# A ring of three h slots and a product with a diagonal of B in the state-space scans of a two-layer Perceiver kernel

## The chip, the cores and the metric

The kernel runs on one core of a Trainium2 chip. Its time is the device time of one execution in microseconds: 3793.17 us as the median of three runs (3791.55, 3793.17, 3795.02). The engines are called PE (TensorE, with PEld for its weight loads), DVE (VectorE), ACT (ScalarE), POOL (GpSimd) and SP (SyncE, which issues the DMAs). Everything is fp32. PSUM is the memory that PE writes; SBUF is the working memory.

## The reference

Two layers, each of cross-attention, a state-space ("Mamba") block and a feed-forward block, over 16 x 64 = 1024 tokens of width 512. What matters here is the recurrence of the two state-space blocks, with 16 states n for each channel d and a restart at each of the 16 sequences of 64 tokens:

```
dA = exp(dt[..., None] * A)
dBx = dt[..., None] * B[:, :, None, :] * x[..., None]
def step(h, inp):
    dA_t, dBx_t, C_t = inp
    h = dA_t * h + dBx_t
    y = jnp.einsum('bdn,bn->bd', h, C_t)
    return (h, y)
y = ys + D * x
```

The block of layer 0 has 512 channels, that of layer 1 has 1024 channels (and multiplies y by a gate after it).

## The kernel before

Channels lie on the 128 partitions and tokens along the free axis. `scan_states` (L220) treats 512 channels, as CN = 4 chunks of 128. It is called three times: once for layer 0 (tile names BS_..., B_...), and for layer 1 once for each half of the channels (ES0 and ES1, shown as ES_..., E_... in the trace). These calls are named the first, second and third scan stage here.

One call runs through 64 steps, in the order half of the tokens (2, HALF = 512 tokens each), state n (16), pair of chunks cp (2). A step s treats W = 2 chunks of 512 tokens, so tiles of 128 x 1024, and goes through four engines:

- ACT makes `dA` = exp(delta * A) in two instructions (L291, 128 x 504 each). It also makes the tile `scaled`: du (that is dt * x), laid out with tokens on partitions in `duT`, times the column B of state n (L272, `times_b`). That is 4 pieces of 128 tokens x 512 channels for each state, which serve the two steps of the state; the list in L294 says how far ahead of the steps the pieces are issued, mostly two after each pair of exponentials.
- PE turns `scaled` back to channels on partitions with 8 transposes of 128 x 128 into the PSUM tile `dB` (`entering`, L365). `dB` has NE = 2 slots, so `entering(s)` waits for scan s-2 (`h_ready`).
- DVE scans: h = dA * h + dB over 1024 elements (`scan`, L329). It writes slot s mod NH of a ring of NH = 2 slots, so scan s waits until POOL has read slot s-2 (`hc_ready`).
- POOL multiplies h by the row C of state n (L315) into a ring `hc` of NP = 2 slots; its step s waits for scan s (`h_ready`) and for PE having added step s-2 (`summed`).
- PE adds `hc` into the PSUM tile `acc`, again with 8 transposes (`add`, L382), after `hc_ready`.

The order on PE is fixed: entering(s+2), then add(s-1). At the last state of each half (n = 15) `add` adds the skip term D * x too (8 more transposes), and DVE finishes the half (`finish`, L340 or L344); in layer 1 ACT copies `acc` out and PE turns it back first (L280, L392). POOL makes the skip terms (L306, four instructions) ahead of its first step. Both rings h and hc lie in the space of `du`, four chunks of 1024 tokens, whose values are no longer needed once `duT` is made.

Of the kernel before, what the change touches and what calls it, by code (L numbers as in the profile page):

```python
# [12 lines left out]
P = 128  # L13
# [180 lines left out]
N_STATE = 16  # L194
HALF = TOK // 2
# [24 lines left out]
def scan_states(nc, consts, tag, delta, du, duT, b_col, A, rows, q0, CN, skip, skip_col, finish_to, gate=None):  # L220

    with ExitStack() as stack:
        r = Region(nc, stack, tag)
        NH, NP, ND, NE, NS = 2, 2, 3, 2, 3
        W = 2
        CP = CN // W
        TILES = HALF // P
        acc = r.ps("acc", [P, CN, HALF])
        dB = r.ps("dB", [P, NE, W, HALF])
        dA = r.sb("dA", [P, ND, W, HALF])  # L230
        h = du[:, 0:2, :].rearrange("p k (w t) -> p k w t", w=W)
        hc = du[:, 2:4, :].rearrange("p k (w t) -> p k w t", w=W)
        scaled = r.sb("scaled", [P, NS, TILES, CN * P])
        yt = r.sb("yt", [P, W, HALF]) if gate is not None else None
        cleared, da_ready, skip_ready = r.sem("cleared"), r.sem("da_ready"), r.sem("skip_ready")
# [8 lines left out]
        def chunks(s):  # L244
            return range(W * STEPS[s][2], W * STEPS[s][2] + W)

        def tokens(tile, c, half):
            return tile[:, c, bass.ts(half, HALF)]

        def ring_q(half, n):  # L250
            return q0 + N_STATE * half + n

        def piece(m, i):
            t = TILES * (m // N_STATE) + i
            return scaled[:, m % NS, i, :], duT[:, t, :], b_col(t, m % N_STATE)

        with nc.Block() as block:
            @block.sync
            def _(sp):
                for k in range(2 * N_STATE):  # L260
                    q = q0 + k + NR
                    if q < rows.total:
                        sp.wait_ge(hc_ready, CP * (k + 1))
                        rows.load_c(sp, q)

            @block.scalar
            def _(act):
                def times_b(m, i):
                    if m >= NS and i == 0:
                        act.wait_ge(db_full, CP * (m - NS + 1))  # L270
                    to, of, col = piece(m, i)
                    nc.scalar.activation(to, of, ACT.Copy, scale=col).then_inc(scaled_ready, 1)  # L272
# [30 lines left out]
            @block.gpsimd  # L303
            def _(pool):
                for c in range(CN):
                    nc.gpsimd.tensor_scalar(skip[:, c, :], skip[:, c, :], skip_col(c), None, ALU.mult  # L306
                                            ).then_inc(skip_ready, 1)
                for s, (half, n, cp) in enumerate(STEPS):
                    q = ring_q(half, n)
                    pool.wait_ge(h_ready, s + 1)  # L310
                    if s >= NP:
                        pool.wait_ge(summed, s - NP + 1)
                    if cp == 0:
                        pool.wait_ge(rows.c_in[q % NR], 16 * (q // NR + 1))
                    nc.gpsimd.tensor_tensor(hc[:, s % NP], h[:, s % NH],  # L315
                                            rows.C[:, q % NR, :].unsqueeze(1).broadcast_to([P, W, HALF]), ALU.mult
                                            ).then_inc(hc_ready, 1)

# [36 lines left out]
            @block.tensor  # L355
            def _(pe):
                def entering(s):
                    half, n, cp = STEPS[s]
                    m = N_STATE * half + n
                    pe.wait_ge(scaled_ready, TILES * (m + 1))  # L360
                    if s >= NE:
                        pe.wait_ge(h_ready, s - NE + 1)
                    for j, c in enumerate(chunks(s)):
                        for i in range(TILES):
                            last = nc.tensor.transpose(dB[:, s % NE, j, bass.ts(i, P)], scaled[:, m % NS, i, bass.ts(c, P)],  # L365
                                                       consts["ident"][:, :])
                    last.then_inc(db_full, 1)

                def add(s):

                    half, n, cp = STEPS[s]
                    pe.wait_ge(hc_ready, s + 1)
                    if half and n == 0:
                        pe.wait_ge(finished, W * (nth_last[s - CP] + 1))
                    for j, c in enumerate(chunks(s)):
                        parts = [hc[:, s % NP, j, :]]
                        if n == N_STATE - 1:
                            pe.wait_ge(skip_ready, CN)
                            parts.append(tokens(skip, c, half))
                        for part in parts:  # L380
                            for i in range(TILES):
                                last = nc.tensor.matmul(acc[:, c, bass.ts(i, P)], part[:, bass.ts(i, P)],  # L382
                                                        consts["ident"][:, :], start=(n == 0 and i == 0),
                                                        stop=(n == N_STATE - 1), is_transpose=True,
                                                        skip_group_check=True)
                    last.then_inc(summed, 1)

                def turn_back(s):
                    for j, c in enumerate(chunks(s)):
                        pe.wait_ge(copied, W * nth_last[s] + j + 1)  # L390
                        for i in range(TILES):
                            last = nc.tensor.transpose(acc[:, c, bass.ts(i, P)], yt[:, j, bass.ts(i, P)],  # L392
                                                       consts["ident"][:, :])
                        last.then_inc(turned, 1)

                for s in range(NE):
                    entering(s)
                for s in range(len(STEPS) + 1):
                    if s + NE < len(STEPS):
                        entering(s + NE)  # L400
                    if s:
                        add(s - 1)
                    if gate is not None and s - 2 in nth_last:
                        turn_back(s - 2)
                for s in LASTS:
                    if gate is not None and s + 2 >= len(STEPS) + 1:
                        turn_back(s)
# [799 lines left out]
def l0_mamba(nc, consts, X, A_log, Dw, xproj, dtw, dtb, bc_scratch, ffn_weights, project):  # L1207
# [3 lines left out]
    with ExitStack() as stack:  # L1211
# [25 lines left out]
        with ExitStack() as inner:  # L1237
# [7 lines left out]
            with nc.Block() as block:  # L1245
# [68 lines left out]
                def _(act):  # L1314
# [19 lines left out]
            q.restart()  # L1334

        scan_states(nc, consts, "BS", delta, du, duT, lambda t, n: Bt[:, t, R + n:R + n + 1], A, rows, 0, CN, XnT,
                    lambda c: Dd[:, c:c + 1], X)
        r.restart()
# [1014 lines left out]
def l1_mamba(nc, consts, X, a, bc_scratch):  # L2353
# [7 lines left out]
    with ExitStack() as stack:  # L2361
# [271 lines left out]
        for g in range(C // CG):  # L2633
            with ExitStack() as inner:
# [11 lines left out]
                with ExitStack() as first:  # L2646
                    acc = first.enter_context(nc.psum_tensor(f"E3{g}_z", [P, CG, TOK], F32))
                    with nc.Block() as block:
# [57 lines left out]
                        def _(dve):  # L2706
# [18 lines left out]
                    q.restart()  # L2725
                chunk = slice(CG * g, CG * g + CG)
                scan_states(nc, consts, f"ES{g}", delta, du, duT, lambda t, n: pr[:, t, R + n:R + n + 1], A[:, chunk, :], rows, 2 * N_STATE * g, CG, U[:, chunk, :],
                            lambda c: cols[:, CG * g + c, Dcol:Dcol + 1], U[:, chunk, :], gate=Gt[:, chunk, :])

# [292 lines left out]
```

## Time and profile before

| | |
|---|---|
| median of three runs | 3793.17 us |
| profiled execution, its own time | 3795.1 us |
| its span | 3793.4 us |
| busy: PE, PEld, DVE, ACT, POOL | 3459.6, 2592.3, 2248.7, 1579.7, 1329.9 us |
| first scan stage, first to last step on POOL | 1100.0 to 1256.2 us |
| second scan stage | 3306.3 us to the last two steps, which start at 3462.15 us |
| third scan stage | 3508.05 to 3666.1 us |

The page gives busy times over the whole span; the attention stages, which the change does not touch, hold most of PE's. The three scan stages make up about an eighth of the span, and they have to be read by themselves, engine by engine. A timeline row merges like instructions that follow each other without a gap: "4.71 ... x2" is 4.71 us from the start of the first to the end of the second, so that the distance of their starts is 4.71 less the length of one. Instructions of an engine may overlap a little in this view: on ACT and PE the next one starts before the one before has ended.

### The profile page before, as it was taken

To read this page: it belongs to the slowest core of one execution; us is meant where nothing else is said; L and a number is where in the kernel's file an instruction comes from. 1 tells how busy PE (TensorE), PEld (TensorE's weight loads), DVE (VectorE), ACT (ScalarE), POOL (GpSimd) and SP (SyncE) were. 2 spreads that over 40 slices of the span, in tenths; PEclk is the share of its full clock that TensorE was granted. 3 is DMA by queue.
4 is the path that set the end of the run, shared out by engine and by line. 5 is a ranking of instruction groups with operands and counts; after the bars stand their busy time and mean duration, and the time that the engine had idled before them with its cause. 6 is when DMAs were issued, how large, how long until landed. Compare 5 with 4: busy or idle time off the path is not lost. (4 is left out here: it accounts for less than half of the span.)

```text
span 3793.4 us, 76745 instructions
## 1 busy us (share of the span) xinstructions
PE 3459.6 (91%) x33752; PEld 2592.3 (68%) x33752; DVE 2248.7 (59%) x2305; ACT 1579.7 (42%) x2169; POOL 1329.9 (35%) x652
## 2 busy tenths in 40 slices
PE   7999999999777689999999999999999998686788
PEld 4566666665247555888888888888888846575764
DVE  4677777777259842555555555555555415597972
ACT  2555555555279421222222222222222103698960
POOL 3344444442069421122222222222222004396961
PEclk9999999999779889999999999999999999798999
DMA  6455555553112042111111111111111112111110
GB/s 203 129 147 151 146 149 149 149 145 86 40 62 54 6 155 78 36 48 34 35 46 42 50 42 50 42 50 42 50 42 46 73 42 56 39 52 34 51 48 23
DMA packets 215251, 277.18 MB, mean 73 GB/s; under 512 B 67056, under 2 KB 165328, under 8 KB 213632
## 3 DMA queue, kind: packets, MB, share of 16 engines
q1 hardware_dynamic: 214920, 272.28, 24.8%
q8 instruction: 267, 4.37, 0.5%
q14 instruction: 64, 0.52, 0.0%
HBM read 218.63 MB, written 53.13 MB: 72 GB/s over the span
## 5 line engine op out<-in xcount | busy, mean ns | idle before, releaser
L1770 POOL TENSOR_TENSOR D_ctx_lo<-D_ctx_raw,D_ctx_hi 128x2048 fp32r<-128x2048 f32 (+1 forms) x64 | 270.0, 4219 | 1203.9 <-ACT D_ctx_hi L1764 1203.9
L730 DVE TENSOR_REDUCE A_mxc<-A_psX 128x2 f32<-128x768 f32 (+2 forms) x512 | 480.8, 983 | 115.5 <-PE A_psX L772 111.6
L1047 ACT ACTIVATE A_probs<-A_psE 128x1024 f32<-128x1024 f32 (+1 forms) x416 | 426.4, 1025 | 294.1 <-PE A_psE L1105 291.9
L1789 ACT ACTIVATE D_V<-D_psY 128x384 f32<-128x384 f32 x208 | 101.9, 490 | 890.0 <-PE D_psY L1855 890.0
L1805 DVE TENSOR_REDUCE D_mxc<-D_psE 128x4 f32<-128x1536 f32 (+2 forms) x128 | 241.9, 1890 | 204.3 <-PE D_psE L1883 204.3
L2146 ACT ACTIVATE D_probs<-D_psE 128x2048 f32<-128x2048 f32 x112 | 210.5, 1879 | 295.8 <-PE D_psE L2259 295.8
L329 DVE TENSOR_TENSOR_SCAN E_du<-ES_dA,ES_dB 128x1024 f32<-128x1024 f32 x128 | 292.3, 2285 | 39.0 <-POOL E_du L315 23.5
L2275 PE MATMUL D_psO<-D_probs,D_V 128*32 128x256 f32 (+1 forms) x5376 | 313.4, 381 | 0.0
L315 POOL TENSOR_TENSOR E_du<-E_du,E_Cn 128x1024 f32<-128x1024 f32 x128 | 301.7, 2373 | 19.2 <-DVE E_du L329 13.1
L1855 PE MATMUL D_psY<-D_wv_hi,D_ctx_hi 128*128 128x384 f32 x832 | 285.5, 343 | 0.0
L1845 PE MATMUL D_psY<-D_ctx_hi,D_wk_hi 128*128 128x384 f32 (+2 forms) x768 | 279.9, 364 | 0.0
L1855 PE MATMUL D_psY<-D_wv_hi,D_ctx_lo 128*128 128x384 f32 x832 | 279.1, 336 | 0.0
L1855 PE MATMUL D_psY<-D_wv_lo,D_ctx_hi 128*128 128x384 f32 x832 | 278.6, 335 | 0.0
L1845 PE MATMUL D_psY<-D_ctx_hi,D_wk_lo 128*128 128x384 f32 (+2 forms) x768 | 268.4, 350 | 0.0
L1845 PE MATMUL D_psY<-D_ctx_lo,D_wk_hi 128*128 128x384 f32 (+2 forms) x768 | 268.4, 349 | 0.0
L2186 DVE TENSOR_TENSOR D_acc<-D_acc,D_probs 128x1024 f32<-128x1024 f32 x96 | 135.7, 1414 | 213.5 <-ACT D_probs L2146 209.8
L2275 PEld LDWEIGHTS D_psO<-D_probs,D_V 128*32 128x32 f32 (+1 forms) x5376 | 163.5, 110 | 115.6 <-issue 9.0
L1105 PEld LDWEIGHTS A_psE<-A_Qst,A_Kst 50*128 50x128 f32 (+1 forms) x1664 | 123.0, 184 | 169.6 <-ACT A_probs L1047 117.4
L1105 PE MATMUL A_psE<-A_Qst,A_Kst 50*128 50x256 f32 (+1 forms) x1664 | 211.4, 333 | 24.9 <-ACT A_probs L1047 19.3
L1120 PE MATMUL A_psO<-A_probs,A_V 128*17 128x256 f32 (+1 forms) x3328 | 228.5, 389 | 0.2 <-ACT A_probs L1047 0.2
L2254 PE MATMUL D_psE<-D_Q_hi,D_K_hi 32*128 32x256 f32 (+1 forms) x2688 | 208.1, 294 | 5.7 <-PEq L49 5.7
L365 PE MATMUL ES_dB<-all_ident,ES_scaled 128*128 128x128 f32 x1024 | 143.0, 286 | 72.2 <-DVE E_du L329 63.6
(368 smaller groups left out, 7654.2 us busy)
## 6 DMA issues: line engine op xcount, KB each, us to landing
A_land<-in_ctx SPq DMA_DIRECT2D x32, 768.0 KB, 5.6
D_ctx_raw<-in_ctx SPq DMA_DIRECT2D x32, 768.0 KB, 4.6
A_land<-in_ctx SPq DMA_DIRECT2D x16, 1024.0 KB, 5.9
D_ctx_raw<-in_ctx SPq DMA_DIRECT2D x16, 1024.0 KB, 5.9
E_Cn<-bc_scratch SPq DMA_DIRECT2D x64, 256.0 KB, 3.3
k_scratch<-A_Khl SPq DMA_DIRECT2D x32, 384.0 KB, 4.3
A_Kst<-k_scratch SPq DMA_DIRECT2D x64, 192.0 KB, 3.5
A_land<-in_ctx SPq DMA_DIRECT2D x16, 642.0 KB, 4.3
```

What stands on the lines that cost most here:

```text
L315: nc.gpsimd.tensor_tensor(hc[:, s % NP], h[:, s % NH], rows.C[:, q % NR, :].unsqueeze(1).broadcast_to([P, W, HALF]), ALU.mult).then_inc(hc ...
L329: nc.vector.tensor_tensor_scan(h[:, s % NH].rearrange("p w t -> p (w t)"), dA[:, s % ND].rearrange("p w t -> p (w t)"), dB[:, s % NE].rear ...
L730: nc.vector.tensor_reduce(mxc[:, u % 4, :, u // 4], psX[:, x % 2, :, 0:w], axis=AX_X, op=ALU.max).then_inc(x_free, 1)
L1047: nc.scalar.activation(probs[0:KW[k], n % NPR, :, :].rearrange("p h q -> p (h q)"), psE[0:KW[k], :], ACT.Exp, scale=HD ** -0.5).then_inc(e ...
L1105: last = nc.tensor.matmul(psE[0:KW[k], col:col + HQ], Kst[j % 2][rows, 2 * g + pair, P * k:P * k + KW[k]], Qst[j % 2][rows, 2 * g + pair, ...
L1120: last = nc.tensor.matmul(psO[32 * h:32 * h + HD + 1, 0:HQ], V[j % 2][0:KW[k], k, HG * g + h, :], probs[0:KW[k], n % NPR, 2 * (h % 2) + h ...
L1770: nc.gpsimd.tensor_tensor(ctx_lo[c][:, :, 0:w], ctx_raw[c][:, :, 0:w], ctx_hi[c][:, :, 0:w].bitcast(F32), ALU.subtract).then_inc(lo_done[c ...
L1805: nc.vector.tensor_reduce(mxc[:, H * a:H * a + H, c], psE[:, :, 0:CH[c][1]], axis=AX_X, op=ALU.max).then_inc(x_free, 1)
L1845: last = nc.tensor.matmul(to[:, 0:w], wk_parts[a][:, d, bass.ts(t, P)], parts[a2][:, d, 0:w], start=(n == 0), stop=(n == len(PASSES) - 1))
L1855: last = nc.tensor.matmul(to[0:KWD[k], 0:H * HD], parts[a][:, d, at], wv_parts[a2][:, d, :], start=(n == 0), stop=(n == len(PASSES) - 1))
L2146: nc.scalar.activation(probs[0:KR, N % NPR, :, :].rearrange("p h q -> p (h q)"), psE[0:KR, :, :].rearrange("p h q -> p (h q)"), ACT.Exp, s ...
L2275: last = nc.tensor.matmul(psO[32 * h:32 * h + 32, t, :], V[0:KWD[k], k, h, bass.ts(t, 32)], probs[0:KWD[k], N % NPR, h, bass.ts(i, NQ)], s ...
```

## The change

- The ring of h gets a third slot (NH = 3), in the space where slot 0 of hc was. Of hc, slot 0 moves to the last chunk of `du` and slot 1 to a new SBUF tile of 128 x 1024. NP stays 2.
- For the last 128 tokens of each half (piece i = 3 of 4), ACT no longer multiplies `duT` (128 x 512) by the column of B, but the identity (128 x 128), so that it makes a diagonal matrix of B. PE then takes, for that piece of each chunk, an fp32 product of `duT` (128 tokens x 128 channels) with this diagonal instead of a transpose. It gives the same 128 x 128 tile of dB. The other three pieces stay as they were.

```
-        NH, NP, ND, NE, NS = 2, 2, 3, 2, 3
+        NH, NP, ND, NE, NS = 3, 2, 3, 2, 3
...
-        h = du[:, 0:2, :].rearrange("p k (w t) -> p k w t", w=W)
-        hc = du[:, 2:4, :].rearrange("p k (w t) -> p k w t", w=W)
+        h = du[:, 0:3, :].rearrange("p k (w t) -> p k w t", w=W)
+        hc = (du[:, 3, :].rearrange("p (w t) -> p w t", w=W), r.sb("hc", [P, W, HALF]))
...
         def piece(m, i):
             t = TILES * (m // N_STATE) + i
+            if diagonal(i):
+                return scaled[:, m % NS, i, 0:P], consts["ident"][:, :], b_col(t, m % N_STATE)
             return scaled[:, m % NS, i, :], duT[:, t, :], b_col(t, m % N_STATE)
+
+        def diagonal(i):
+
+            return i >= TILES - 1
...
-                            last = nc.tensor.transpose(dB[:, s % NE, j, bass.ts(i, P)], scaled[:, m % NS, i, bass.ts(c, P)],
-                                                       consts["ident"][:, :])
+                            to = dB[:, s % NE, j, bass.ts(i, P)]
+                            if diagonal(i):
+                                last = nc.tensor.matmul(to, duT[:, TILES * half + i, bass.ts(c, P)], scaled[:, m % NS, i, 0:P],
+                                                        start=True, stop=True)
+                            else:
+                                last = nc.tensor.transpose(to, scaled[:, m % NS, i, bass.ts(c, P)], consts["ident"][:, :])
```

The remaining two edits only index the ring hc as a pair of tiles. On PE, the start of the first scan stage (its second `entering`, then the fourth, with the first `add`) reads as follows before the change; "x7" counts the seven transposes behind the first, BS_dB is the output of `entering`, BS_acc that of `add`.

```order
L365 MATMUL BS_dB<-all_ident,BS_scaled 128x128 [waits BS_scaled_ready]
L365 MATMUL BS_dB<-all_ident,BS_scaled 128x128 x7
L365 MATMUL BS_dB<-all_ident,BS_scaled 128x128 [waits BS_h_ready,BS_scaled_ready]
L365 MATMUL BS_dB<-all_ident,BS_scaled 128x128 x7
L382 MATMUL BS_acc<-all_ident,B_du 128x128 [waits BS_hc_ready]
L382 MATMUL BS_acc<-all_ident,B_du 128x128 x7
```

The same place in the changed kernel, from the fourth `entering` on, where L373 is the product and B_duT its stationary operand:

```order
L376 MATMUL BS_dB<-all_ident,BS_scaled 128x128 [waits BS_h_ready,BS_scaled_ready]
L376 MATMUL BS_dB<-all_ident,BS_scaled 128x128 x2
L373 MATMUL BS_dB<-BS_scaled,B_duT 128x128
L376 MATMUL BS_dB<-all_ident,BS_scaled 128x128 x3
L373 MATMUL BS_dB<-BS_scaled,B_duT 128x128
L392 MATMUL BS_acc<-all_ident,BS_hc 128x128 [waits BS_hc_ready]
L392 MATMUL BS_acc<-all_ident,BS_hc 128x128 x7
```

Two of the eight transposes of `entering` have become products; the waits stand where they stood. On DVE the scans of the first scan stage, before (-) and after (+), from its first step:

```order
-L329 SCALAR_TENSOR_TENSOR B_du<-BS_dA,BS_dB 128x1024 [waits BS_db_full,BS_da_ready] x2
-L329 SCALAR_TENSOR_TENSOR B_du<-BS_dA,BS_dB 128x1024 [waits BS_hc_ready,BS_db_full,BS_da_ready] x32
+L335 SCALAR_TENSOR_TENSOR B_du<-BS_dA,BS_dB 128x1024 [waits BS_db_full,BS_da_ready] x3
+L335 SCALAR_TENSOR_TENSOR B_du<-BS_dA,BS_dB 128x1024 [waits BS_hc_ready,BS_db_full,BS_da_ready] x31
```

On ACT, the first pieces and exponentials of that stage before the change:

```order
L272 ACTIVATE BS_scaled<-B_duT,B_Bt 128x512 x4
L291 ACTIVATE BS_dA<-B_delta,B_A 128x8x63 [waits BS_cleared]
L291 ACTIVATE BS_dA<-B_delta,B_A 128x8x63
L272 ACTIVATE BS_scaled<-B_duT,B_Bt 128x512 x4
L291 ACTIVATE BS_dA<-B_delta,B_A 128x8x63 x2
```

and in the changed kernel, where every fourth piece is the diagonal:

```order
L278 ACTIVATE BS_scaled<-B_duT,B_Bt 128x512 x3
L278 ACTIVATE BS_scaled<-all_ident,B_Bt 128x128
L297 ACTIVATE BS_dA<-B_delta,B_A 128x8x63 [waits BS_cleared]
L297 ACTIVATE BS_dA<-B_delta,B_A 128x8x63
L278 ACTIVATE BS_scaled<-B_duT,B_Bt 128x512 x3
L278 ACTIVATE BS_scaled<-all_ident,B_Bt 128x128
L297 ACTIVATE BS_dA<-B_delta,B_A 128x8x63 x2
```

The number of ACT's instructions stays; one piece in four is four times narrower. On DVE it is thus: three scans instead of two go ahead without waiting for POOL, and each later one waits for a POOL step that lies one further back.

## Rows read from the trace of the kernel before

**Rows 1.** The page: busy time of each engine; two groups of the scan.

```profile
PE 3459.6 (91%) x33752; PEld 2592.3 (68%) x33752; DVE 2248.7 (59%) x2305; ACT 1579.7 (42%) x2169; POOL 1329.9 (35%) x652
...
L329 DVE TENSOR_TENSOR_SCAN E_du<-ES_dA,ES_dB 128x1024 f32<-128x1024 f32 x128 | 292.3, 2285 | 39.0 <-POOL E_du L315 23.5
...
L315 POOL TENSOR_TENSOR E_du<-E_du,E_Cn 128x1024 f32<-128x1024 f32 x128 | 301.7, 2373 | 19.2 <-DVE E_du L329 13.1
```

**Rows 2.** Timeline, steady scan: start us, us, engine line op, [idle before].

```profile
3332.13 4.62 DVE L329 TENSOR_TENSOR_SCAN E_du<-ES_dA,ES_dB 128x1024 f32<-128x1024 f32 x2 [0.25 <-POOL E_du L315]
...
3334.49 4.71 POOL L315 TENSOR_TENSOR E_du<-E_du,E_Cn 128x1024 f32<-128x1024 f32 x2 [0.16 <-DVE E_du L329]
...
3334.56 1.06 PE L365 MATMUL ES_dB<-all_ident,ES_scaled 128*128 128x128 f32 x8 [0.60 <-DVE E_du L329]
...
3335.46 1.04 PE L382 MATMUL ES_acc<-all_ident,E_du 128*128 128x128 f32 x8
...
3337.00 4.62 DVE L329 TENSOR_TENSOR_SCAN E_du<-ES_dA,ES_dB 128x1024 f32<-128x1024 f32 x2 [0.25 <-POOL E_du L315]
```

**Rows 3.** Timeline of ACT near the start of the second scan stage.

```profile
3311.09 1.32 ACT L291 ACTIVATE ES_dA<-E_delta,E_A 128x504 f32<-128x504 f32 x2
...
3313.55 1.31 ACT L291 ACTIVATE ES_dA<-E_delta,E_A 128x504 f32<-128x504 f32 x2
...
3319.84 1.33 ACT L291 ACTIVATE ES_dA<-E_delta,E_A 128x504 f32<-128x504 f32 x2 [1.31 <-DVE E_du L329]
```

**Rows 4.** L315 by stage: ns min/median/max, first and last start us.

```profile
L315 POOL TENSOR_TENSOR E_du<-E_du,E_Cn x128: 2344/2373/2392, 3306.3 to 3666.1; 128x1024 f32<-128x1024 f32 x128
L315 POOL TENSOR_TENSOR B_du<-B_du,B_Cn x64: 2348/2371/2389, 1100.0 to 1256.2; 128x1024 f32<-128x1024 f32 x64
```

**Rows 5.** Timeline of POOL in the first scan stage (BS).

```profile
1107.89 4.70 POOL L315 TENSOR_TENSOR B_du<-B_du,B_Cn 128x1024 f32<-128x1024 f32 x2 [0.69 <-PE BS_acc L382]
...
1171.19 7.25 POOL L315 TENSOR_TENSOR B_du<-B_du,B_Cn 128x1024 f32<-128x1024 f32 x3 [0.16 <-DVE B_du L329]
...
1187.68 4.71 POOL L315 TENSOR_TENSOR B_du<-B_du,B_Cn 128x1024 f32<-128x1024 f32 x2 [1.00 <-DVE B_du L329]
```

**Rows 6.** Timeline of POOL in the second (ES0) and third stage (ES1).

```profile
3315.00 4.70 POOL L315 TENSOR_TENSOR E_du<-E_du,E_Cn 128x1024 f32<-128x1024 f32 x2 [1.49 <-PE ES_acc L382]
...
3378.34 4.71 POOL L315 TENSOR_TENSOR E_du<-E_du,E_Cn 128x1024 f32<-128x1024 f32 x2 [0.17 <-DVE E_du L329]
...
3396.12 4.71 POOL L315 TENSOR_TENSOR E_du<-E_du,E_Cn 128x1024 f32<-128x1024 f32 x2 [0.98 <-DVE E_du L329]
...
3462.15 4.68 POOL L315 TENSOR_TENSOR E_du<-E_du,E_Cn 128x1024 f32<-128x1024 f32 x2 [0.17 <-DVE E_du L329]
...
3508.05 4.68 POOL L315 TENSOR_TENSOR E_du<-E_du,E_Cn 128x1024 f32<-128x1024 f32 x2
```

**Rows 7.** Groups of ACT by shape: busy us, mean ns of one.

```profile
L272 ACT ACTIVATE ES_scaled<-E_duT,E_pr 128x512 f32<-128x512 f32 x256 | 169.7, 717 | 1.2 <-PEq L49 1.2
...
L1544 ACT ACTIVATE C_xi<-C_xi,C_rsi 128x256 f32<-128x256 f32 x8 | 4.1, 509 | 6.8 <-DVE C_rsi L1472 6.8
...
L2691 ACT ACTIVATE E_early<-E_cols 128x1 f32<-128x1 f32 x2 | 0.4, 202 | 0.0
```

**Rows 8.** Timeline of PE where fp32 products and transposes alternate.

```profile
3695.43 0.60 PE L184 MATMUL E_acc<-all_ident,E_n_xn 128*128 128x128 f32 x4
3695.87 7.03 PE L2763 MATMUL E_acc<-E_wout,E_U 128*128 128x512 f32 x16
```

**Rows 9.** Windows of L2826: PE busy (records), PEld busy (records), PEclk, DMA share, GB/s.

```profile
3742.00:3744.00 2.00, 2.00 (x20) 2.00 (x19) 1.00 0.03 8
```

**Rows 10.** Windows: busy (instructions) of PE, PEld, DVE, ACT, POOL; PEclk, DMA share, GB/s.

```profile
3310.00:3313.00 3.00, 2.46 (x13) 2.09 (x12) 2.96 (x2) 2.86 (x6) 2.83 (x2) 0.50 0.18 62
3322.00:3400.00 78.00, 63.28 (x527) 57.04 (x528) 72.25 (x36) 75.33 (x125) 72.46 (x32) 1.00 0.20 53
```

**Rows 11.** Timeline of PE at the start of the second stage.

```profile
3311.21 1.94 PE L365 MATMUL ES_dB<-all_ident,ES_scaled 128*128 128x128 f32 x8 [0.54 <-DVE E_du L329]
```

More of the change, by code:

```diff
@@ L314, in _ @@
                         pool.wait_ge(rows.c_in[q % NR], 16 * (q // NR + 1))
-                    nc.gpsimd.tensor_tensor(hc[:, s % NP], h[:, s % NH],
+                    nc.gpsimd.tensor_tensor(hc[s % NP][:, :, :], h[:, s % NH],
                                             rows.C[:, q % NR, :].unsqueeze(1).broadcast_to([P, W, HALF]), ALU.mult
@@ L375, in add @@
                     for j, c in enumerate(chunks(s)):
-                        parts = [hc[:, s % NP, j, :]]
+                        parts = [hc[s % NP][:, j, :]]
                         if n == N_STATE - 1:
```

## Prediction

> **What bounds the kernel now.** I read the page first, then the timeline of the scan stages engine by engine. The page names PE as the busiest engine, but that is an average over the attention stages, which the change leaves alone; its two scan groups show that DVE and POOL, each with 128 steps in layer 1, are both busy nearly all of the scan [rows 1]. So the question is what paces a scan step.
>
> The timeline of the steady scan shows a beat of 4.87 us for two steps: DVE starts a pair at 3332.13 and the next at 3337.00 [rows 2]. That is 2.435 us for a step. Two things have just this length.
>
> First, the ring of two h slots. One scan takes 2.285 us, one POOL step 2.373 us [rows 1]. The first scan of the pair at 3332.13 ends at 3334.42; POOL starts on it at 3334.49 and ends at 3336.86; DVE's next pair, which writes that slot again, starts at 3337.00 [rows 2]. 2.29 + 0.07 + 2.37 + 0.14 = 4.87: a closed loop over two steps. Both waits in it are visible, 0.25 us on DVE and 0.16 us on POOL for each two steps.
>
> Second, ACT. At the start of the second stage ACT is behind and waits for nothing: from 3311.09 to 3313.55 it does two exponentials and two pieces, so 2.46 us for a step's four instructions, about 0.61 us each although one lasts 0.71 us. Only at 3319.84 does it wait for DVE, once [rows 3]. ACT's own floor is thus 2.44 to 2.46 us for a step, the same as the ring's. Either one alone would keep the beat, and a change that removes one of them gains nothing.
>
> The next floors lie close below. DVE: a pair of scans takes 4.62 us, less one of 2.285, gives a distance of 2.335 us. POOL: 4.71 less 2.373 gives 2.337 us [rows 1, 2]. PE: `entering` and `add` need 16 transposes of 0.11 us (below), 1.76 us.
>
> How far POOL is from its floor, in total: its first and last steps lie at 3306.3 and at 3464.5 (3462.15 plus 2.34) in the second stage, 3508.05 and 3666.1 in the third, 1100.0 and 1256.2 in the first, so 158.2 + 158.0 + 156.2 = 472.4 us for 3 x 63 = 189 distances [rows 4, 6]. At 2.337 us they would be 441.7 us. 30.7 us is all that POOL waits in the scans, and the most that the change can give, since nothing makes a POOL step shorter.
>
> **The change, part by part.** *The third h slot.* Scan s waits for POOL step s-3 instead of s-2. The loop is then 4.87 us over three steps, 1.62 us, and no longer sets the beat. It adds no wait. The second tile of hc is only another place for the same bytes.
>
> *The diagonal piece on ACT.* One piece in four shrinks from 512 to 128 columns. No row shows it. A piece of 512 lasts 0.717 us, the like instruction with 256 columns 0.509 us, one with a single column 0.202 us [rows 7]. The first two give 0.81 ns a column, so 0.41 us for 128; less the 0.10 us by which neighbours overlap, it takes 0.30 us of ACT. Bounds: 0.10 us (0.202 less 0.10) and 0.61 us (as before). I take 0.30, the value nearest to the 256-column row. ACT's state, two steps, is then 4.87 - 0.61 + 0.30 = 4.56 us, 2.28 us for a step: just under 2.337. It would set the beat again only from 0.42 us up.
>
> *The product on PE.* A step has two of them. Where fp32 products of 512 columns stand beside transposes, 16 records (8 products, each in two records) take 7.03 us, 0.88 us a product, and four transposes take 0.44 us, from 3695.43 to 3695.87 [rows 8]. A quarter of the width makes 0.22 us, against 0.11 for the transpose it replaces. Products of 137 columns agree: 20 records in 2.00 us at the full clock, 0.20 to 0.23 us a product, their weight loads beside them [rows 9]. So PE gains 0.22 us a step, 1.98 us in all, below 2.337. The way from the end of a scan to the full dB grows from 1.20 us (3334.42 to 3335.62) to 1.4 us, and dB's two slots allow 2.335 us for it, so it stays hidden. Upper bound: 0.29 us for each of the two records, no overlap, which is a product of 0.58 us.
>
> *What is late next.* POOL and DVE, both at 2.336 us. They do not disturb each other: they already overlap nearly always, and POOL's steps spread only from 2344 to 2392 ns [rows 4]. At the start of a stage POOL is late (it makes the skip terms first) and DVE can now run three scans ahead, so DVE enters the steady part about 2 us ahead of POOL's need, which covers small disturbances. I allow 0.01 us a step for waits that stay, 1.9 us in all.
>
> *What stays of the other waits.* At the start POOL waits 1.49 us for PE in the second and third stage and 0.69 us in the first [rows 5, 6]: PE's clock is at 0.50 there, 1.2 GHz, and eight transposes take 1.94 us instead of 1.06 [rows 2, 10, 11]. The products cost double there too, while the third slot lets one `entering` go earlier; I leave the 3.7 us as they are. At the change of halves, POOL's steps 29 to 35 take 17.78 us in layer 1 (3378.34 to 3396.12), 3.2 more than six steady steps (14.61), and 16.49 us in the first stage (1171.19 to 1187.68), 1.9 more [rows 5, 6]. In layer 1 this is a chain (add, copy, turn back, finish) of which nothing gets shorter and in which two scans stand behind a `finish`: DVE's lead is used up in it. I put 3.5 us there. In layer 0 there is no copy; DVE's 2.4 us of `finish` are covered by its lead, and I put 0.4 us.
>
> *The sum.* 30.7 - 3.7 (starts) - 7.0 (halves, layer 1) - 0.4 (half, layer 0) - 1.9 = 17.7 us. The profiled execution took 3795.1 us, 1.9 above the median of the runs, so 3795.1 - 17.7 = 3777.4 there, and 3775.5 us on the scale of the median.
>
> The Trainium skill ("TensorE: Matmul & The Clock Gate", Terms) says that the transpose mode is four times faster for fp32. By that rule a product would cost 0.44 us. The rows make it twice, not four times; what the rule would do is the second rival.
>
> **The rivals.** *ACT stays the bound.* The small piece costs almost what the large one did, because the fixed part of an instruction is large: at 0.61 us nothing changes, 3793 us; at 0.50 us ACT would be at 2.38 us a step, and the gain 0.055 x 174 steady steps + 1.5 = 11 us, 3782 us. For it: a single column already lasts 0.202 us. Against: the 256-column row is 0.21 us shorter than the 512-column one.
>
> *PE becomes co-bound at a fourfold product.* 14 x 0.11 + 2 x 0.44 = 2.42 us a step; the beat would go from 2.435 to 2.42, a gain of 2.6 us over 174 steps and some at the halves, about 3790 us. Against: rows 8 and 9. This is the time that the rule above gives.
>
> *PE becomes the bound, and the kernel slower.* Each `entering` goes four times between transpose and product. If each change cost the 0.16 us by which a lone transpose (0.27 us) is longer than its distance to the next, PE would need 1.98 + 0.66 = 2.64 us a step, and 174 steps would lose 0.2 us each: 3793 + 36 = 3829 us. It decides from 0.11 us a change on, where PE passes 2.435. Against: the first transpose behind products and the first product behind transposes show no gap [rows 8]; but there a wide product hides the loads.
>
> *No change where the trace shows none:* a further wait of the same length as the two (ACT's uneven steps, one with two full pieces and one with a full and a small one, or PE's fixed order) holds the beat near 2.40. The gain would be 6 to 8 us, 3786 us. For it: four engines would lie within 0.36 us of each other. Against: every ring but h has a step to spare in the rows read.
>
> **How the numbers follow.** Forecast 0.76; ACT stays near the bound 0.07; PE fourfold 0.04; PE slower 0.05; another wait 0.08. 0.2% is 7.6 us, about what a measurement of this kernel can tell: faster means below 3785.6, slower above 3800.8. The forecast and half of the first rival fall below, as does a third of the last: 0.84 faster. The rest of them and the fourfold product are no change: 0.11. Slower 0.05. The forecast's own range: if DVE's lead covers the halves wholly and no wait stays, the gain is 27 us; if the beat is 2.36 instead of 2.347, it is 15; with a diagonal of 0.45 us on ACT, 14. The range of 3768 to 3787 takes these in, and reaches to the mild cases of the rivals.
>
> **What would show it.** In the changed profile: POOL's steps 2.337 us apart in long rows without waits; its stage lengths about 152.8 us in layer 1 and 148.9 us in the first stage; DVE's waits for POOL nearly gone in the steady part; L278's 128-column form at 0.41 us; two records of the product at about 0.11 us distance. The prediction is wrong if steady steps stay over 2.39 us, and the engine without any idle time there then names the rival: ACT, or PE with waits of DVE for dB behind it.

## The result

The changed kernel takes 3772.1 us (median of four runs, 3768.6 to 3775.3), the kernel before on the same chip 3792.4 us (3787.6 to 3795.0). The ratio is 0.9948, with an interval of 0.9931 to 0.9965: 19.7 us less by the ratio, or 0.5%. The forecast was 3775.5 us, in a range of 3768 to 3787.

The profiled execution took 3775.3 us (span 3773.5), 19.9 us less in its span than before. In the page of the changed kernel, the lines that answer to [rows 1] are these:

```profile
PE 3505.6 (93%) x34136; PEld 2644.1 (70%) x34136; DVE 2240.0 (59%) x2305; ACT 1549.3 (41%) x2169; POOL 1324.5 (35%) x652
...
L335 DVE TENSOR_TENSOR_SCAN E_du<-ES_dA,ES_dB 128x1024 f32<-128x1024 f32 x128 | 287.6, 2277 | 20.0 <-PE ES_dB L373 12.0
```

ACT has 30.4 us less work, PE 46.0 us more. Scans wait for POOL no longer: the 23.5 us of [rows 1] have gone. What is left in layer 1 is 12.0 us of waits for PE's dB, most of it for the first dB of a stage, and 4.5 us of waits for ACT. The steps on POOL (L321 now; one slot of hc lies in `du` and the other in its own tile, so the steps have two names), by stage, from the view of one line:

```profile
L321 POOL TENSOR_TENSOR E_du<-E_du,E_Cn x64: 2349/2382/2503, 3299.7 to 3642.2; 128x1024 f32<-128x1024 f32 x64
L321 POOL TENSOR_TENSOR ES_hc<-E_du,E_Cn x64: 2354/2384/2506, 3302.0 to 3644.5; 128x1024 f32<-128x1024 f32 x64
L321 POOL TENSOR_TENSOR B_du<-B_du,B_Cn x32: 2358/2380/2414, 1095.3 to 1241.5; 128x1024 f32<-128x1024 f32 x32
L321 POOL TENSOR_TENSOR BS_hc<-B_du,B_Cn x32: 2361/2380/2425, 1097.6 to 1243.8; 128x1024 f32<-128x1024 f32 x32
```

A step lasts no less than before [rows 4], but it follows its predecessor sooner. POOL's timeline in the second stage (start, us, engine, line):

```profile
3327.88 2.40 POOL L321 TENSOR_TENSOR E_du<-E_du,E_Cn 128x1024 f32<-128x1024 f32 x1
3330.22 2.39 POOL L321 TENSOR_TENSOR ES_hc<-E_du,E_Cn 128x1024 f32<-128x1024 f32 x1
3332.55 2.40 POOL L321 TENSOR_TENSOR E_du<-E_du,E_Cn 128x1024 f32<-128x1024 f32 x1
...
3374.46 2.49 POOL L321 TENSOR_TENSOR E_du<-E_du,E_Cn 128x1024 f32<-128x1024 f32 x1
3377.32 2.39 POOL L321 TENSOR_TENSOR ES_hc<-E_du,E_Cn 128x1024 f32<-128x1024 f32 x1 [0.37 <-PE ES_acc L392]
3381.21 2.38 POOL L321 TENSOR_TENSOR E_du<-E_du,E_Cn 128x1024 f32<-128x1024 f32 x1 [1.50 <-DVE E_du L335]
3384.58 2.38 POOL L321 TENSOR_TENSOR ES_hc<-E_du,E_Cn 128x1024 f32<-128x1024 f32 x1 [0.99 <-DVE E_du L335]
```

The beat is 2.33 us, where it was 4.87 for two [rows 2]. Behind the first steps of a stage only the change of halves (the last four rows) still has waits. From POOL's first to its last step the three stages take 148.5, 150.15 and 149.9 us (from 156.2, 158.2 and 158.0 in [rows 4 to 6]), together 448.6 instead of 472.4: 23.8 us less. The span gives only 19.9 of them; where 3.9 us went is told below.

ACT and PE in the steady part, each in its timeline, first ACT:

```profile
3330.24 0.71 ACT L278 ACTIVATE ES_scaled<-E_duT,E_pr 128x512 f32<-128x512 f32 x1
3330.85 0.39 ACT L278 ACTIVATE ES_scaled<-all_ident,E_pr 128x128 f32<-128x128 f32 x1
3331.15 1.31 ACT L297 ACTIVATE ES_dA<-E_delta,E_A 128x504 f32<-128x504 f32 x2
```

```profile
3330.33 1.09 PE L392 MATMUL ES_acc<-all_ident,E_du 128*128 128x128 f32 x8
3331.26 0.49 PE L376 MATMUL ES_dB<-all_ident,ES_scaled 128*128 128x128 f32 x3
3331.59 0.39 PE L373 MATMUL ES_dB<-ES_scaled,E_duT 128*128 128x128 f32 x2
3331.81 0.49 PE L376 MATMUL ES_dB<-all_ident,ES_scaled 128*128 128x128 f32 x3
3332.14 0.39 PE L373 MATMUL ES_dB<-ES_scaled,E_duT 128*128 128x128 f32 x2
3332.66 1.09 PE L392 MATMUL ES_acc<-all_ident,ES_hc 128*128 128x128 f32 x8
```

The diagonal piece lasts 0.39 us and the next instruction starts 0.30 us after it. The product is two records 0.11 us apart (from 3331.59 to 3331.81), and there is no gap where transposes and products alternate.

### The profile page after: what moved, and what is told of

Same layout as the page of the kernel before. It is cut to its first block and busy times, and to the rows that moved or that the text cites. A ratio compares the mean times of both kernels' runs of the same rounds, so it can differ in the third digit from the quotient of the medians.

```text
span 3773.5 us, 77513 instructions
## 1 busy us (share of the span) xinstructions
PE 3505.6 (93%) x34136; PEld 2644.1 (70%) x34136; DVE 2240.0 (59%) x2305; ACT 1549.3 (41%) x2169; POOL 1324.5 (35%) x652
## 5 line engine op out<-in xcount | busy, mean ns | idle before, releaser
L709 POOL TENSOR_TENSOR A_ctx_lo<-A_land,A_ctx_hi 128x1536 fp32r<-128x1536 f32 (+2 forms) x60 | 199.1, 3319 | 4.8
L2264 PE MATMUL D_psE<-D_Q_hi,D_K_lo 32*128 32x256 f32 (+1 forms) x2688 | 196.8, 277 | 0.0
```

The lines of the kernel that those rows point to most:

```text
L2264: nc.tensor.matmul(psE[0:KWD[k], h, bass.ts(i, NQ)], lhs[rows, t, K0[k]:K0[k] + KWD[k]], rhs[rows, t, :], start=(t == 0 and lhs is K_parts ...
```

## The experiments

Twelve kernels were run. All are edits of the changed kernel's `scan_states`. "Steps" are mean distances of POOL's starts in us in the second stage, read from its timeline. Each ratio is against the kernel before on the same chip, whose median lay between 3791.0 and 3795.2 us; so times of different rows are compared to within a few us only.

| kernel | time, us | ratio to before | steps 7 to 29; from 40 on |
|---|---|---|---|
| changed kernel | 3772.1 | 0.9948 (0.9931 to 0.9965) | 2.331; 2.330 |
| ring of three, no diagonal | 3773.9 | 0.9953 (0.9941 to 0.9966) | 2.332; 2.403 |
| diagonal, ring of two | 3801.5 | 1.0022 (1.0012 to 1.0032) | 2.443; 2.447 |
| diagonal for every second state | 3772.5 | 0.9948 (0.9934 to 0.9961) | 2.330; 2.330 |
| two diagonal pieces of four | 3772.4 | 0.9947 (0.9934 to 0.9961) | 2.331; 2.326 |
| three | 3790.9 (one run) | | 2.431; 2.427 |
| four | 3829.4 | 1.0091 (1.0076 to 1.0106) | 2.660; 2.645 |
| POOL 896 wide | 3744.1 (one run) | | 2.176; 2.217 |
| DVE 896 wide | 3771.2 (one run) | | 2.331; 2.330 |
| both 896 wide | 3740.0 (one run) | | 2.128; 2.247 |
| finish one step later | 3776.4 | 0.9951 (0.9935 to 0.9968) | 2.334; 2.330 |
| skip products on DVE | 3759.9 | 0.9914 (0.9893 to 0.9935) | 2.332; 2.328 |
| ring of three, no diagonal, skip on DVE | 3772.3 | 0.9946 (0.9927 to 0.9965) | 2.407; 2.401 |

### The two parts of the change, each alone

```
         def diagonal(i):
-            return i >= TILES - 1
+            return False
```

> Only the third h slot; all four pieces stay transposes. Theory: ring and ACT had the same 2.435 us a step, so ACT (2.44 us a step) keeps the beat and DVE shows waits for ACT's dA: steady steps 2.43 to 2.44 us, 3792 us (3788 to 3795). Rival 1 (the ring alone did it, ACT only followed): steps at 2.33, 3772 us.

Measured: 3773.9 us, the rival's time. By the medians the ring alone gives all but 2 us of the gain, and the intervals of the two ratios overlap; the three stages on POOL are 4.3 us longer in sum than in the changed kernel (149.5, 151.7 and 151.7 us). The forecast's sentence on this case was wrong. The trace shows both why ACT's floor is real and why it hardly mattered. ACT begins the second stage at 3288.45 and is busy all the time from there to its last exponential; its first row, and a window of 74 us with the columns of [rows 10], whose fourth pair is ACT:

```profile
3288.45 2.56 ACT L278 ACTIVATE ES_scaled<-E_duT,E_pr 128x512 f32<-128x512 f32 x4 [0.62 <-PEq L49]
```

```profile
3300.00:3374.00 74.00, 62.58 (x494) 54.79 (x494) 69.08 (x31) 74.00 (x123) 74.00 (x32) 0.96 0.19 54
```

DVE's timeline in the second stage:

```profile
3335.04 2.29 DVE L335 TENSOR_TENSOR_SCAN E_du<-ES_dA,ES_dB 128x1024 f32<-128x1024 f32 x1 [0.16 <-ACT ES_dA L297]
3337.49 2.29 DVE L335 TENSOR_TENSOR_SCAN E_du<-ES_dA,ES_dB 128x1024 f32<-128x1024 f32 x1 [0.17 <-ACT ES_dA L297]
3339.94 2.29 DVE L335 TENSOR_TENSOR_SCAN E_du<-ES_dA,ES_dB 128x1024 f32<-128x1024 f32 x1 [0.16 <-ACT ES_dA L297]
```

and POOL's, somewhat later:

```profile
3407.86 2.37 POOL L321 TENSOR_TENSOR ES_hc<-E_du,E_Cn 128x1024 f32<-128x1024 f32 x1
3410.20 2.37 POOL L321 TENSOR_TENSOR E_du<-E_du,E_Cn 128x1024 f32<-128x1024 f32 x1
3412.64 2.37 POOL L321 TENSOR_TENSOR ES_hc<-E_du,E_Cn 128x1024 f32<-128x1024 f32 x1
3415.08 2.39 POOL L321 TENSOR_TENSOR E_du<-E_du,E_Cn 128x1024 f32<-128x1024 f32 x1
```

From 3335 on DVE goes at ACT's 2.45 us. POOL still goes at 2.33, eating DVE's lead of two scans at 0.11 us a step; at the change of halves it loses 3.1 us and with that wins the lead back; only from 3410 on is it down to ACT's 2.44, for some 15 steps.

```
-        NH, NP, ND, NE, NS = 3, 2, 3, 2, 3
+        NH, NP, ND, NE, NS = 2, 2, 3, 2, 3
```

> Only the diagonal piece; two h slots. Theory: the loop scan, POOL, scan over two slots stays at 4.87 us for two steps: 2.435 us a step, ACT now with idle time of 0.3 us for two steps, 3792 us (3788 to 3795). Rival 2 (ACT's relief alone did it): steps at 2.33, 3772 us.

Measured: 3801.5 us, 0.22% slower than before and outside the 3788 to 3795 that was expected, though the beat is the expected one. It is that of [rows 2] again, in DVE's timeline:

```profile
3331.00 4.66 DVE L335 TENSOR_TENSOR_SCAN E_du<-ES_dA,ES_dB 128x1024 f32<-128x1024 f32 x2 [0.21 <-POOL ES_hc L321]
3335.87 4.67 DVE L335 TENSOR_TENSOR_SCAN E_du<-ES_dA,ES_dB 128x1024 f32<-128x1024 f32 x2 [0.21 <-POOL ES_hc L321]
```

So the ring of two sets 4.87 us whatever ACT needs. The stages are 157.5, 159.3 and 159.1 us long, 3.5 more in sum than before. The places are those where PE is late: at the start POOL waits 1.92 us for PE (1.49 and 0.69 in [rows 5, 6]), and steps 29 to 35 take 18.23 instead of 17.78 us in layer 1. That fits a dearer product where no lead hides it, but no run takes the product away by itself. The other half of the slowdown (3.7 of the profiled execution's 7.2 us) lies between the stages, in code that is the same, and stays unexplained.

### How much of the diagonal is needed, and what a product costs

```
-            return i >= TILES - 1
+            return i >= TILES - 1 and m % 2 == 1
```

> Three h slots, but the diagonal piece only in every second state, so half of ACT's relief. Theory: ACT sets the beat by its sum, 15 instructions of 0.61 us and one of 0.30 for four steps: 2.36 us a step, 0.027 more than with every state, 3777 us (3774 to 3780). Rival 1 (ring alone): 3772 us, steps at 2.333.

3772.5 us, POOL's steps at 2.33: ACT at (2.44 + 2.28)/2 = 2.36 us a step, above POOL's 2.33, costs nothing that can be measured. A miss of the same kind as the first: 3777 us (3774 to 3780) was expected.

```
-            return i >= TILES - 1
+            return i >= TILES - 2      (and - 3, - 4)
```

> Three h slots, two of the four pieces are diagonals. ACT falls to about 2.13 us a step, PE rises to 20 records of 0.11, 2.2 us. Theory: POOL and DVE hold 2.333 us, nothing more is gained: 3772 us (3769 to 3775). Rival (ACT still sets the beat after the change): steps fall below 2.333 and the time by up to 10 us.

> Three of four pieces are diagonals: 12 product records, 2 transposes and 8 transposes in a step, 22 of 0.1085 us. Theory: PE just passes POOL and DVE: 2.39 to 2.42 us a step, 3783 to 3790 us. Rival (PE's waits for both neighbours add up before its sum reaches 2.333): 2.45 us or more.

> Three h slots, all four pieces are diagonals, no transpose is left in the entering of a step: 16 product records and 8 transposes, 24 of 0.1085 us. Theory (a product is two records of 0.11 us and changing between product and transpose is free): PE sets the beat, 2.60 to 2.64 us a step, 3792 + 0.2 x 189 = 3830 us (3820 to 3838). Rival (a product costs four transposes): 8 x 0.44 + 0.87 = 4.4 us a step, over 4100 us. Rival (PE hides more than its records show): under 3800 us.

3772.4, 3790.9 and 3829.4 us. With two, POOL still holds the beat. With three, the one run and its steps of 2.43 us lie just above what was expected (3790 us and 2.42). With four, the steps of 2.66 us lie just above the expected 2.64, PE has no idle time from 3330 to 3370 us, and it shows the price of a product most cleanly (its timeline):

```profile
3340.18 1.95 PE L373 MATMUL ES_dB<-ES_scaled,E_duT 128*128 128x128 f32 x16
3341.97 1.04 PE L392 MATMUL ES_acc<-all_ident,ES_hc 128*128 128x128 f32 x8
3342.84 1.95 PE L373 MATMUL ES_dB<-ES_scaled,E_duT 128*128 128x128 f32 x16
```

Sixteen records (eight products) from 3340.18 to 3341.97 are 1.79 us, 0.22 us a product; eight transposes from 3341.97 to 3342.84 are 0.11 us each. Their sum, 2.66 us, is the distance of POOL's steps. For three pieces 10 x 0.11 + 6 x 0.22 = 2.42 us; measured 2.43. The Trainium skill ("TensorE: Matmul & The Clock Gate", Terms) gives the transpose mode as four times faster for fp32. In this stream it is twice as fast, and the measurement decides: by four, a step with four pieces would have taken 4.4 us. Every transpose and every record of a product here has a weight load of its own, and the rows don't tell which of the two sets the 0.11 us.

### What bounds the changed kernel

The next three leave 64 tokens of each chunk out of POOL's product, of the scan, or of both, so their output isn't the reference's.

```
-        W = 2
+        W, CUT = 2, 448
...
-                    nc.gpsimd.tensor_tensor(hc[s % NP][:, :, :], h[:, s % NH],
+                    nc.gpsimd.tensor_tensor(hc[s % NP][:, :, 0:CUT], h[:, s % NH, :, 0:CUT],
```

> As after, but POOL multiplies only 448 of the 512 tokens of each chunk and half (the rest of the product with C is left out). POOL's step is about 2.05 us. Theory (DVE's floor is the same as POOL's, 2.333): steps stay at 2.33. Rival (POOL alone sets the beat): steps fall to ACT's 2.285.

> As after, but DVE scans only 896 of 1024 elements (the rest of h is left out). The scan is about 2.0 us. Theory: POOL holds 2.333. Rival (DVE alone sets the beat): steps fall to ACT's 2.285.

> Both of the last two cuts together (POOL 448 of 512 tokens, DVE 896 of 1024 elements; the rest is left out). Theory: the next floor is ACT's, 2.28 to 2.29 us a step (seven instructions of 0.61 us and one of 0.30 us for two steps); a stage of 63 distances is about 3 us shorter than after the change. Rival (PE at 1.98 us or something not seen): steps below 2.2 us, or at 2.33 still.

POOL narrower: 3744.1 us, with steps of 2.18 and later 2.22 us. This was a miss: the forecast had DVE at the same 2.335 as POOL, and the steps fell below the rival's 2.285 too. DVE's timeline with the narrow POOL step shows its own floor:

```profile
3324.79 26.21 DVE L336 TENSOR_TENSOR_SCAN E_du<-ES_dA,ES_dB 128x1024 f32<-128x1024 f32 x12
```

Twelve scans in 26.21 us, the last 2.26 long: 23.95 / 11 = 2.18 us. The narrow POOL step isn't what makes DVE faster: with the ring alone, where POOL's product is whole, the last three scans of the second stage start at 3444.47, 3446.68 and 3448.85, 2.21 and 2.17 us apart. The 2.335 us of [rows 2] was POOL's pace, passed on to DVE through the ring. DVE narrower alone (3771.2 us) changes nothing (POOL's steps stay at 2.331). With both narrower (3740.0 us) the steps are 2.06 us while the lead lasts, 2.13 on average over steps 7 to 29, and then DVE shows what comes next:

```profile
3381.64 4.14 DVE L336 TENSOR_TENSOR_SCAN E_du<-ES_dA,ES_dB 128x896 f32<-128x896 f32 x2 [0.42 <-ACT ES_dA L297]
3386.20 4.14 DVE L336 TENSOR_TENSOR_SCAN E_du<-ES_dA,ES_dB 128x896 f32<-128x896 f32 x2 [0.42 <-ACT ES_dA L297]
3390.76 4.14 DVE L336 TENSOR_TENSOR_SCAN E_du<-ES_dA,ES_dB 128x896 f32<-128x896 f32 x2 [0.42 <-ACT ES_dA L297]
```

4.56 us for two steps, each pair waiting for ACT: the 2.28 us of the forecast for ACT with one diagonal piece. But the second stage is 141.4 us long, 8.8 less than the changed kernel's where 3 were expected: as with the ring alone, POOL's late start gives ACT a lead, and its floor comes into force only late. The floors of the changed kernel are thus POOL 2.33, ACT 2.28 and DVE 2.18; PE's 1.98 is a sum of its records (14 x 0.11 + 2 x 0.22), since no run with one diagonal piece is paced by PE.

### The change of halves

```
-                    if s - 3 in nth_last:
-                        finish(s - 3)
+                    if s - 4 in nth_last:
+                        finish(s - 4)
```

> As after, but DVE finishes a half one scan later (finish(s-4) in place of finish(s-3)), so that one more scan stands before the wait for PE's turned tiles. Theory (in layer 1 the change of halves costs 3.1 us because DVE stands 2.9 us in its finish): POOL's steps 29 to 35 take 15.5 to 16.2 us instead of 17.1, 2 to 3 us less in all, 3770 us. Rival (the chain add, copy, turn, finish, add sets it whatever DVE does): 17.1 us as before or more.

3776.4 us (3775.9 to 3778.3), no gain, as the rival had it. Steps 29 to 35 take 17.67 us in the second stage and 16.14 in the first, where the changed kernel has 17.09 and 14.38. The timelines of PE, of ACT and of DVE there say what happened:

```profile
3380.03 1.04 PE L402 MATMUL ES_acc<-all_ident,ES_yt 128*128 128x128 f32 x8
...
3383.31 1.06 PE L392 MATMUL ES_acc<-all_ident,E_du 128*128 128x128 f32 x8 [1.15 <-DVE E_U L350]
...
3387.10 1.06 PE L392 MATMUL ES_acc<-all_ident,ES_hc 128*128 128x128 f32 x8 [0.74 <-DVE E_U L350]
```

```profile
3377.38 1.09 ACT L286 ACTIVATE ES_yt<-ES_acc 128x512 f32<-128x512 f32 x2 [4.03 <-PE ES_acc L392]
```

```profile
3379.70 2.29 DVE L335 TENSOR_TENSOR_SCAN E_du<-ES_dA,ES_dB 128x1024 f32<-128x1024 f32 x1 [1.96 <-ACT ES_dA L297]
```

The first `add` of the new half waits for the `finish` that empties `acc`, and PE's later work stands behind that `add`. DVE's wait for the turned tiles (2.93 us in the changed kernel) has gone, but its next scan waits 1.96 us for ACT, whose exponentials stand behind the copy of `acc`, and that copy waited 4.03 us for PE's last `add`. The wait has moved to PE and ACT, not gone.

### The start of a stage

The last pair moves POOL's four skip products (11.32 us before its first step) to DVE, three into DVE's idle time before the first scan and one behind the second.

```
-                for c in range(CN):
-                    nc.gpsimd.tensor_scalar(skip[:, c, :], skip[:, c, :], skip_col(c), None, ALU.mult
-                                            ).then_inc(skip_ready, 1)
...
+                def skips(cs):
+                    for c in cs:
+                        nc.vector.tensor_scalar(skip[:, c, :], skip[:, c, :], skip_col(c), None, ALU.mult
+                                                ).then_inc(skip_ready, 1)
+                skips(range(CN - 1))
...
                 for s in range(len(STEPS)):
                     scan(s)
+                    if s == 1:
+                        skips([CN - 1])
```

> The changed kernel, with its four skip products (11.32 us on POOL at a stage's start) done by DVE instead: three in its idle 4.6 us before the first scan, one behind the second scan. Theory (POOL alone bounds the scans, from its first product to its last step, and at the start it is late by the 11.3 us): POOL's first step begins about 7.2 us after the stage's start instead of 11.3, the steps after it follow the scans and ACT (2.28 us a step) and then stand 2.33 apart; DVE has no lead of three scans at first, so the change of halves costs the first stage up to 1.5 us more. 3 to 4 us less a stage, 3762 us in all (3759 to 3766), which beats both kernels. Rival (the start is set by PE at the low clock and by ACT's first pieces, POOL's products are hidden behind them): no more than 1 us a stage, 3769 to 3772.

> The ring of three without the diagonal, with the skip products moved to DVE in the same way. Theory (ACT's 2.44 us a step is a real floor, and the ring alone gained 18 us only because ACT works from the stage's start and POOL begins 11.3 us later, so that ACT's lead of some 11 us is eaten at 0.11 us a step; at the end of a stage ACT already sets the beat): POOL starts 4 us earlier but its steps stand 2.44 apart nearly from the start, ACT ends when it did, and so does the stage: 3773 us (3771 to 3776), the same as the ring alone. The diagonal is then worth 10 us where it was worth 2. Rival (ACT's floor is lower than 2.44 and POOL sets the time): it gains as much as the same edit does on the changed kernel, 3763 to 3765 us, with POOL's steps 2.33 apart.

Both times came out as expected: 3759.9 and 3772.3 us. On the changed kernel the edit gains some 12 us, and it is the fastest version here that gives the reference's output (ratio 0.9914). The first stage's change of halves didn't get dearer (14.39 us). Without the diagonal the same edit gains nothing that can be measured (3773.9 to 3772.3): in its second stage POOL starts 7.1 us after the stage's first instruction instead of 11.3, but DVE waits for ACT almost at once. DVE's timeline there:

```profile
3333.72 2.29 DVE L339 TENSOR_TENSOR_SCAN E_du<-ES_dA,ES_dB 128x1024 f32<-128x1024 f32 x1 [0.16 <-ACT ES_dA L297]
3336.16 2.29 DVE L339 TENSOR_TENSOR_SCAN E_du<-ES_dA,ES_dB 128x1024 f32<-128x1024 f32 x1 [0.15 <-ACT ES_dA L297]
```

POOL's steps are 2.44 apart here (3333.64, 3336.09, 3338.53), and its stage is 155.9 us long instead of 151.7: what was won at the start is lost on the way. From the first instruction of a stage (ACT's first piece) to the start of POOL's last step, the timelines give, in us:

| kernel | first stage | second | third |
|---|---|---|---|
| changed kernel | 159.8 | 161.5 | 161.2 |
| skip products on DVE | 155.2 | 158.0 | 157.9 |
| ring of three, no diagonal | 160.8 | 163.0 | 163.0 |
| the same, skip on DVE | 160.9 | 163.0 | 163.0 |

The edit takes 11.5 us from the stages where ACT has the diagonal, and nothing (0.1 us at most) where it hasn't; there ACT has no idle time before its last exponential in either kernel. So by the medians the diagonal is worth 2 us while POOL starts late, and 12 us (3772.3 to 3759.9) once it doesn't; by the stages 4.3 and 15.7.

## Why the prediction was right, and where it was wrong

**The mechanism and the sign held.** The ring of two was the beat, the third slot took it away, and POOL became the bound. The diagonal's 0.30 us on ACT, the product's two records of 0.11 us, the missing gap between products and transposes and ACT's 2.28 us were all measured as forecast. The rivals of a fourfold product and of a gap at each change are refuted by the product's rows: two records 0.11 us apart, and no gap beside transposes. The one with ACT as the bound and the one with another wait near 2.40 are refuted by POOL's 2.33.

**The step that failed: "Either one alone would keep the beat, and a change that removes one of them gains nothing."** For the ring this holds (the diagonal alone gained nothing, and lost 9 us); for ACT it doesn't. Two chains of 64 steps run side by side, but they don't begin together. ACT begins with the stage, at 3288.45 in the run with the ring alone, and has 64 x 2.44 us and four copies of 0.6, until 3447.0 (3446.9 in its timeline); the exponentials of its last three steps come in one row, POOL follows them at its own pace, and its last step starts at 3451.46. POOL begins 11.3 us later, at 3299.77, and by itself would need 63 x 2.333 + 3.1 us, until 3449.9 (3449.88 in the changed kernel). The two chains end within 2 us of each other. A floor of 2.44 against one of 2.333 costs 0.107 x 63 = 6.7 us, and POOL's late start hides all but 1.0 to 1.8 us of it in each stage. The two runs with the skip products on DVE show it: with the late start gone, POOL's chain is 4 us earlier and ACT's isn't. The forecast compared costs a step and left out where each chain starts. It reached the right time all the same, since the change has both parts; that this step did no harm to the number is luck.

**"The next floors": DVE's wasn't 2.335.** That was a distance in a chain that POOL held, not DVE's own: that is 2.18 us. It changed no term here, since POOL is as slow as was said, but the text said that two engines tie, and they don't.

**The terms of the sum.** The scans gained 23.8 us where 17.7 was forecast, 6 more. Steady steps: 2.331 us instead of 2.337 plus 0.01 for residual waits, 174 steps x 0.016 = 2.8 us. Starts: POOL waits 1.36 us for PE in the first stage (0.69 before) and 0.17 and 0.1 in the others, 1.6 in sum where 3.7 were kept: 2.1 us. Halves: steps 29 to 35 take 14.38, 17.09 and 16.96 us, 0.4 + 3.1 + 3.0 over six steady steps, where 7.4 were kept: 0.9 us. These are the 6 us but for 0.3. The time came out within 3.4 us of the forecast in part because two misses of opposite sign met: 6 us more won in the scans, and 3.9 us lost outside them, for which the sum had no term.

**What was given back.** 3.9 of the 23.8 us don't reach the span. At the end of the first stage the granted clock falls: 0.64 in the window from 1245 to 1248 us, 1.00 at that place before, and from POOL's last step to the first instruction of the next block it takes 7.77 us instead of 6.74. In the third stage the clock falls at the product behind the scan; the windows there, after and before (columns as in [rows 10]), are

```profile
3652.00:3655.00 3.00, 1.79 (x3) 0.90 (x4) 0.47 (x1) 0.00 (x0) 0.00 (x0) 0.76 0.27 60
3655.00:3658.00 3.00, 3.00 (x6) 1.14 (x6) 0.00 (x0) 0.00 (x0) 0.00 (x0) 0.68 1.00 392
```

```profile
3673.00:3676.00 3.00, 1.43 (x5) 0.68 (x4) 1.02 (x2) 0.00 (x0) 0.00 (x0) 1.00 0.15 16
3676.00:3679.00 3.00, 3.00 (x8) 1.33 (x7) 0.00 (x0) 0.00 (x0) 0.00 (x0) 1.00 0.97 356
```

The wide product behind the scan runs its first windows at 0.76 and 0.68 instead of 1.00, and the way from POOL's last step to the end of the kernel is 129.0 us instead of 127.3. From the second stage's last POOL step to the third one's first it is 44.69 us instead of 43.58. That makes 3.8 us with the 1.0 of the first stage.

The traces of the other runs say how far the clock accounts for it. Behind the first stage, only the changed kernel and the one with the later finish have the fall, and they need 7.8 to 7.9 us to the next block, all the others 6.5 to 6.8. Behind the third stage, seven traces have a stretch of 3.4 us at a clock of 0.50 that begins 8.3 to 9.2 us after the start of POOL's last step, and need 128.3 to 129.3 us to the end; the six without any need 126.9 to 128.2 (one has it at 0.6 us, and needs 127.7). So each fall goes with about 1 us. The second stage's end isn't explained so: 43.5 to 44.4 us without the fall, 44.1 to 44.7 with it (the two kernels with the skip products on DVE left out, where POOL starts earlier). What brings the fall on stays open. It would be near at hand that DVE is three scans ahead at a stage's end, so that PE has no `entering` left beside the last two `add`s and idles longer (its busy time in the window from 1239 to 1242 us is 1.66 us). But the ring alone, with the same three slots, shows no such fall behind any stage, and the diagonal with a ring of two shows one behind the third. The unchanged code ahead of the first stage was 4.7 us faster in this execution and that between the first and second 4.8 us slower (without the 1.0); these cancel here, and they show how far one execution can be read.

**Sums that don't come out.** The chance of "faster" that follows from the text is 0.76 + 0.035 + 0.027 = 0.82, not 0.84, and that of no change 0.13. Four changes at 0.16 us are 0.64 us, not 0.66. A gain of 27 us would have been 3766.2 us on the scale of the median, just outside the stated range. None of these touches the forecast.

## What to carry to other kernels

Where two engines seem to need the same time for a step, don't ask only which is slower a step, but also when each one's chain begins: work that one engine does before its first step (here 11.3 us) is a lead for the others, and a floor 0.1 us higher may cost little over 63 steps (here 1 to 1.8 us of 6.7 a stage). For the same reason look at what stands ahead of the loop on the engine that bounds it: moving it to an engine that is idle then gained some 12 us, three fifths of what the change itself gained. And a steady distance is the floor of one engine only; the others merely show it too.

## What the runs showed of the hardware

The multiplication of 128 x 1024 fp32 elements by a column takes POOL 2.84 us and DVE 0.73 us. Where it ran on DVE beside a POOL step, that step became longer. POOL and DVE in the fastest version, each by its timeline:

```profile
3285.36 2.37 POOL L318 TENSOR_TENSOR E_du<-E_du,E_Cn 128x1024 f32<-128x1024 f32 x1 [48.57 <-DVE E_du L339]
3287.68 2.82 POOL L318 TENSOR_TENSOR ES_hc<-E_du,E_Cn 128x1024 f32<-128x1024 f32 x1
3290.54 2.36 POOL L318 TENSOR_TENSOR E_du<-E_du,E_Cn 128x1024 f32<-128x1024 f32 x1
```

```profile
3279.57 0.75 DVE L329 TENSOR_SCALAR E_U<-E_U,E_cols 128x1024 f32<-128x1024 f32 x1
3282.99 4.46 DVE L339 TENSOR_TENSOR_SCAN E_du<-ES_dA,ES_dB 128x1024 f32<-128x1024 f32 x2 [2.67 <-PE ES_dB L379]
3287.37 0.90 DVE L329 TENSOR_SCALAR E_U<-E_U,E_cols 128x1024 f32<-128x1024 f32 x1
```

2.82 us instead of 2.37, and 0.90 instead of 0.75 on DVE; the same in the first stage (2.83 and 0.90). Without the diagonal, where the two start 0.16 us apart, POOL's step takes 2.79 us and DVE's product 0.73. POOL's steps beside scans stay at 2.37 us there. The Trainium skill ("Trainium Architecture — The Big Picture", What this means for kernel authors) says that DVE and GpSimd share a pair of ports and that this is "an exclusive lock (not a bandwidth split)"; the rows agree in that the two hinder each other at this instruction, POOL by 0.45 us once a stage; whether by a lock they don't show.

Not expected either: POOL's steps get longer, from 2.37 to 2.50 us, in parts of the changed kernel's stages (2.49 at 3369.81, and the next one starts at 3372.13), and their distance stays at 2.33. So the length of such a step in the trace isn't what it costs; the distance is.
